# Weight jobs of the attention stage: issued at the beginning of each group, converted at other steps

## The reference

```python
xn = _layernorm(x)
qkv = clip(xn @ Wqkv.T, -8, 8); q, k, v = split(qkv); q = layer_norm(q); k = layer_norm(k)
scores = q @ k.T / 4 + slope[head] * (key position - query position)    # causal
s = (softmax(scores) @ v) @ Wout.T
W = (imatrix - zeros) * scales                                          # gate, up, down; 512 x 1792
g = silu((silu(xn @ W_gate) * (xn @ W_up)) @ W_down)
out = x + s * g
```

## Time and profile before

| | |
|---|---|
| median of 3 runs | 1126.78 us (1124.39 to 1127.07) |
| the profiled execution: its own time | 1119.51 us |
| its span, first to last instruction | 1117.7 us |
| PE busy | 1039.0 us, 93% |
| DVE busy | 933.7 us, 84% |
| ACT busy | 722.6 us, 65% |
| POOL busy | 465.6 us, 42% |
| chain that ended last: PE | 30% of the span, the other engines 3% or less each |

### The profile page before, as it was taken

The page is one execution under the profiler, slowest core; times in us unless marked ns, Lnnn a source line. Parts: engine busy times, 40 slices in busy tenths (PEclk is TensorE's granted clock), DMA queues, the critical chain, the costliest instruction groups (busy, mean ns, idle before and its releaser), DMA issues. The chain is left out here.

```text
span 1117.7 us, 18980 instructions
## 1 busy us (share of the span) xinstructions
PE 1039.0 (93%) x6242; PEld 639.5 (57%) x6242; DVE 933.7 (84%) x2162; ACT 722.6 (65%) x1152; POOL 465.6 (42%) x554
## 2 busy tenths in 40 slices
PE   5999987998999999989999999899999999999995
PEld 4788764433344343433444333577778778777874
DVE  6778897887888787878889885579989998998896
ACT  3666655675767666666667668567747766774774
POOL 2566545221111111111121112039946864994686
PEclk9999999999999998999999999899999999999997
DMA  6254862543544544464454343100120011012001
GB/s 214 70 158 137 220 149 78 154 123 64 142 109 109 129 78 97 90 142 109 95 125 94 103 87 106 39 1 0 40 75 1 1 49 66 1 39 76 1 1 38
DMA packets 98584, 95.32 MB, mean 85 GB/s; under 512 B 28030, under 2 KB 80950, under 8 KB 98486
## 3 DMA queue, kind: packets, MB, share of 16 engines
q1 hardware_dynamic: 96854, 93.72, 32.7%
q10 hardware_dynamic: 1632, 0.39, 0.2%
HBM read 72.45 MB, written 21.23 MB: 84 GB/s over the span
## 5 line engine op out<-in xcount | busy, mean ns | idle before, releaser
L896 ACT ACTIVATE pr<-pair 128x1024 f32<-128x1024 f32 (+3 forms) x384 | 296.6, 813 | 168.1 <-PE pair L1017 90.7
L279 DVE CUSTOM_DVE_ANT_0 bank<-bank,sg 128x384 f32<-128x384 f32 (+3 forms) x488 | 231.4, 517 | 73.4 <-PE bank L289 72.1
L1538 PE MATMUL pair<-xc_lo,w_gu 128*128 128x512 f32 x448 | 182.6, 408 | 4.1 <-DVE xc_lo L1374 4.1
L1539 PE MATMUL pair<-xc_hi,w_gu 128*128 128x512 f32 x448 | 176.5, 394 | 0.0
L282 DVE TENSOR_REDUCE mx<-bank 128x1 f32<-128x512 f32 x240 | 150.5, 684 | 6.0 <-PE bank L289 3.7
L1386 DVE SCALAR_TENSOR_TENSOR gate<-pair,sgu,gate 128x512 f32<-128x512 f32 x168 | 124.5, 741 | 27.0 <-PE pair L1539 25.4
L1177 POOL TENSOR_TENSOR yt<-yt,tmp 128x512 f32<-128x512 f32 x96 | 124.2, 1314 | 0.0
L289 PE MATMUL bank<-ks,qs 108*128 108x512 bf16 (+3 forms) x384 | 116.2, 335 | 5.6 <-DMA ks<-in_krows 5.0
L1012 PE MATMUL pair<-s_sb,xin_c 111*128 111x512 bf16 (+3 forms) x384 | 97.8, 338 | 12.0 <-DMA s_sb<-dt 9.2
L289 PE MATMUL bank<-xin_c,s_sb 108*128 108x512 bf16 (+3 forms) x344 | 106.0, 341 | 3.1 <-DMA xin_c<-in_krows 3.0
L1012 PE MATMUL pair<-qs,ks 111*128 111x512 bf16 (+3 forms) x384 | 97.1, 337 | 12.7 <-DMA qs<-dt 11.0
(11 more groups left out here) (122 smaller groups left out, 2166.5 us busy)
## 6 DMA issues: line engine op xcount, KB each, us to landing
stk<-parts SPq DMA_DIRECT2D x16, 768.0 KB, 5.7
zst<-in_z_all SPq DMA_DIRECT2D x24, 448.0 KB, 4.0
sst<-in_w_all SPq DMA_DIRECT2D x24, 448.0 KB, 5.7
xin_c<-in_x SPq DMA_DIRECT2D x32, 256.0 KB, 3.3
s_sb<-stk SPq DMA_DIRECT2D x96, 64.0 KB
xin_c<-stk SPq DMA_DIRECT2D x96, 64.0 KB
qs<-stk SPq DMA_DIRECT2D x96, 64.0 KB
ks<-stk SPq DMA_DIRECT2D x96, 64.0 KB
```

Source lines behind the costliest of these rows:

```text
L279: dve.tensor_tensor_reduce(out=src, in0=src, in1=tri[:, 512 - w:512], scale=1.0, scalar=-3.0e38, op0=ALU.add, op1=ALU.max, accum_out=dst). ...
L896: act.activation(pr[e % 3][:, 2 * p:2 * p + 2, 0:w], pair[p][:, :, 0:w], ACT.Exp, scale=SCALE)\
L1538: pe.matmul(GB[j % 4], w, xc_lo[:, k, :], start=True, stop=False)
L1539: pe.matmul(GB[j % 4], w, xc_hi[:, k, :], start=False, stop=True).then_inc(gu_done, 1)
```

## The change

The three half jobs of a pair of groups are given to other places. Before, in an even group: SP issues half job 1 (it waits for POOL's job 0), and ACT converts half job 0 at step 6. In an odd group: SP issues half job 2 and then half job 0 of the next pair, and ACT converts job 1 at step 2 and job 2 at step 6. After: each group but the first begins on SP with half job `s` of its pair, an odd group then issues half job 2, and ACT converts job `s` at step 3 and, in odd groups, job 2 at step 8. POOL's jobs go with them: job `s` stands behind the first chain, job 2 behind the second. In the last group SP issues the loads of stage three ahead of half job 2.

```diff
-        JOB_AT, JOB1_AT = 6, 2
+        JOB_AT, JOB2_AT = 3, 8
...
                 def body(i, s, ip, last):
-                    if s == 1:
-                        half_job(ip, 2)
-                    if not last:
-                        half_job(*((ip, 1), (ip + 1, 0))[s])
-                    else:
+                    if i > 0:
+                        half_job(ip, s)
+                    if last:
...
                         sp.dma_start(oin_v[0:DN, 0:P], s_all[4 * KT:, :].rearrange("h (i p) -> (h i) p", p=P)).then_inc(sdn_in, 16)
+                    if s == 1:
+                        half_job(ip, 2)
                     if last is None:
...
                 def body(i, s, ip, last):
-                    if s == 1:
-                        job(ip, 1)
-
                     pool.wait_ge(m_free, number(i, of_kind["own"][-1]) + 1)
...
                     chain(pool, mx0[:, :, :], 2 * i + 1)
-                    job(ip, (0, 2)[s])
+                    job(ip, s)
...
                         chain(pool, mx1[:, 0, :, :], 2 * i + 2)
+                    if s == 1:
+                        job(ip, 2)
...
-                        if e == JOB1_AT and s == 1:
-                            convert(ip, 1)
                         if e == JOB_AT:
-                            convert(ip, (0, 2)[s])
+                            convert(ip, s)
+                        if e == JOB2_AT and s == 1:
+                            convert(ip, 2)
```

## The result

The changed kernel is slower. Its median is 1191.72 us (1190.95 to 1192.36, 4 runs) against 1126.92 (1124.39 to 1129.40, 4 runs): a ratio of 1.0575, 95% interval 1.0550 to 1.0599. The forecast was 1198, with 1160 to 1232 as its range. The profiled execution took 1191.35 us, its span is 1189.6 us. Of all runs reported here two were in a slow state, one of e1 (1678.78 us) and one of e8 (3498.36 us): they stand in the medians of these two, but not in the ratios.

A forecast was written before the change was run, and what follows sets the result against it. PE was taken to set the pace, standing still only for DMAs. Stall 39, clock 29, job 2 2 and last group 1.5 sum to 71.5 us; on 1119.5 that gives 1191, plus 7.3 gives 1198, range 1160 to 1232.

The forecast's parts named there:

- values issued: On SP's queue, behind the lower-half loads: the values are issued 9.4 us after the D1 send.
- values to landing: From issue of the values to the half job's landing: 6.8 us, with 4.7 for `sst` and 1.1 for the values' data.
- PE resumes step 4: PE can start step 4 at 18.9 us after the D1 send, where it would otherwise start at 13.15.
- PE's stall, each group: PE stands still 5.75 us before step 4 in groups 1 to 14; against waits removed, +39 us in fourteen.
- group without any wait: Length of a stage-two group without DMA waits and clock loss: 29.67 us, against 32.61 in the kernel before.
- clock, each group: PE's granted clock falls behind each stall: 2.1 us a group, +29 us in all, from 0 to 3.0 a group.
- length of a group: Distance of D1 sends in stage two: about 37.6 us, against 32.61 in the kernel before.
- tail: Last group: job 2 is loaded about 5 us later and ACT meets it at step 8, +1.5 us (0 to 3).
- Job 2 at step 8: Odd groups: transfer over before D0, conversion costs 0.3 us each, +2 in all; rival, collision with D0: 1225, chance 0.10.
- The clock did not stay up: Rival that the clock stays up: same stall, but PE catches up or half speed costs nothing; 1169 us, chance 0.13.
- The draw: Rival: data about 13 us after the send, PE stall some 2.5 us replaces the removed waits; 1127 us, chance 0.04.
- The other side: Rival: half job is there in time for step 3, only the 41 us gain is left; 1089 us, chance 0.06.

The follow-up runs named there:

- e1: Changed kernel with ACT's conversions at steps 6 and 11 instead of 3 and 8: 1107.08 us, ratio 0.9875 to the kernel before.
- e8: Kernel before with the half jobs' loads cut to 16 of 896 columns, all but the first job's: 1090.89 us, ratio 0.9691.
- e2: Changed kernel with the first conversion at step 5 instead of 3, the second still at 8: 1118.33 us, ratio 0.9963 to the kernel before.
- e10: Changed kernel with 21 unneeded matmuls in front of step 4 of groups 1 to 14: 1167.14 us, ratio 1.0358 to the kernel before.
- e6: Changed kernel with 15 unneeded matmuls in front of step 4 of groups 1 to 14: 1181.04 us, ratio 1.0495 to the kernel before.
- e3: Changed kernel with the first conversion at step 4 instead of 3, the second still at 8: 1127.05 us, ratio 1.0041 to the kernel before.
- e4: Changed kernel with SP issuing the next group's half job between upper-half and lower-half loads, not behind the values: 1087.11 us, ratio 0.9697 to the kernel before.
- e5: Changed kernel with the next group's half job issued in front of the values instead of behind them: 1178.45 us, ratio 1.0476 to the kernel before.
- e9: Kernel before with SP's half job moved from in front of the upper-half loads to between them and the lower-half loads: 1096.81 us, ratio 0.9743.
- e12: e9 with the half job behind the wait for step 11's scores and odd groups' step 2 conversion at step 3: 1088.16 us, ratio 0.9649.
- e11: e4 run again, on the same chip as e9: 1088.17 us, ratio 0.9658 to the kernel before.

## Why the prediction was right

Point by point, "us after the send" as in the prediction:

| step | predicted | measured |
|---|---|---|
| values issued | 9.4 | 9.13 (mean of 14, 8.63 to 10.07) |
| values to landing | 6.8 | 6.6 (18.42 - 2.7 - 9.13) |
| PE resumes step 4 | 18.9 | 18.42 (17.44 to 19.95) |
| PE's stall, each group | 5.75 | 4.75 (66.5 / 14) |
| group without any wait | 29.67 | 29.63 to 29.66 (e2, six groups) |
| step 4 to the next send, no clock lost | 16.52 | 16.52 (e2, even groups), 16.88 (e10) |
| clock, each group | 2.1 | 2.1 (19.02 - 16.88, e10), 1.5 (e6) |
| length of a group | 37.6 | 37.44 |
| tail | +1.5 | +4.0 |
| sum, span | +71.5 | +71.9 |

- **The mechanism** was the forecast's: e3, e2 and e1 move only the conversion and take the loss away step by step; e4 moves only the load and takes it away whole. The landing was sized rightly as a sum, with two parts wrong in opposite ways: data of the values ahead cost 0.1 us and not 1.1 (e5), and `sst` landed in 5.0 us and not 4.7. The estimate from the Trainium skill's price for a DMA ("DMA: Bandwidth & Descriptors", section "Anatomy of one DMA"), which would have put the forecast at 1169, was too short, as the row said: `sst` took 4.4 us at the least here too.
- **The stall** was 1.0 us a group too long in the forecast. PE resumed 0.5 us earlier, and it came to its stop later: at 13.67 us after the send (18.42 - 4.75), not 13.15. 0.16 of that is the end of the last piece's pipeline, which the start of step 4 in the earlier trace rows hides, and 0.28 are DMA waits that had not quite gone (4.0 us in 14 groups), which I had counted as zero. The stall as the profile gives it is therefore not the whole delay: step 4 starts 5.3 us later than the 13.15 of the forecast.
- **What made up for it.** The length of a group is 18.42 us to step 4 and 19.02 from there to the next send. The forecast had 18.9 and, with its 2.1 for the clock and 0.15 for job 2, 18.8 (29.67 - 13.15 + 2.1 + 0.15). So the second part came out 0.25 us longer. The clock is 2.14 of it (e10). The conversion at step 8 costs 0.23 us in odd groups, where 0.3 stood: in e4 they take 16.75 us from step 4 to the send, even ones 16.52. Another 0.26 us a group comes behind a stall even when the clock stays up (e10 has 16.78 in even and 17.02 in odd groups); the forecast had no such term, and its cause stays open. That the sum agrees to half a microsecond is luck; that the terms agree within 1 us a group is not.
- **The miss that is left.** The span grew by 71.9 us where the sum said 71.5, and yet the forecast of 1198 is 6 us above the median. That is the 7.3 us by which the median lay above the profiled execution of the kernel before: in the changed kernel the profiled execution, 1191.35, is 0.4 us below the median.
- **Job 2 at step 8** did not collide with D0 in groups 1 to 14, as forecast, because the stall itself kept them apart: half job 2 went out 7.5 to 9.0 us ahead of D0 in the seven odd groups. In e2, with the stall gone, they met. In the last group, which has no stall, they met too, and that is the term of the tail that was sized at 1.5 and measured 4.0.
- **The rivals.** The clock did not stay up (it would have been worth 30 us by e10, where the prediction said 29). The draw exists, with the conversion at step 4 (e3). The other side, the job there in time, was priced at 1089; e4, which makes it so, took 1087.11, and by its ratio to the kernel before on its chip it would be 1093 here.

## What to carry to other kernels

"At the beginning of an iteration" on an in-order queue means behind all that the iteration before still has to issue: look up in the trace when that place comes, and only then choose where the consumer waits. In this kernel the load that nobody needed soon did best behind the small transfer on which the busiest engine waits, and behind the loads that are needed next, not in front of them. If a stall of TensorE can't be removed, its price is the stall and the clock behind it, here 4.75 and 2.1 us; most of the second part could be bought back with matmuls whose results nobody reads (24.6 us of some 30).

## What was not expected of the hardware

- D1 and D0, 12 KB each on ACT's queue, were late when a half job was issued on SP's queue just before or together with them: D0 took 5.2 us from its issue with a half job issued 0.7 us ahead of it (e2), D1 4.6 us with one issued 0.08 us after the start of its own issue (e9), and with the half job 1.4 us or more behind (e12) it was waited for 0 to 1.06 us, where PE gets to it 2.3 us after the send. Not each half job issued together with a send did this: in one group of e4, of e11 and of e9, with `zst` 0.06 or 0.07 us behind the start of the send, PE waited less than 0.3 us.
- More matmuls made the kernel faster: 294 of them, 24.6 us (e10).
- Between groups with 1.2 to 1.5 us of stall left and those with 1.8 to 2.4, the time differed by more than the stall, 2.3 us in the mean in e6 (35.4 and 37.7), with the granted clock at 1.00 in the first and 0.50 for some microseconds in the second.
